# A four-layer graph network on one core: the fourth layer's states in two float32r terms, with edits to the start, the histogram, the reload and the layer ends

## The reference

```
x = layernorm(x + L0)   # mean over incoming edges of (x[src] + rel_emb[type64]) @ W_msg.T + b_msg, plus x @ W_self.T + b_self
x = layernorm(x + L1)   # 4-head attention: exp(att) * weight, summed over dst for each src, then normed per head
x = layernorm(x + L2)   # sum over incoming edges of x[src] @ (W_data or W_control).T, plus self term, relu
x = layernorm(x + L3)   # out[src] += (x[dst] @ W.T + b) / sqrt(deg[src] * deg[dst]), self loops added
```

## Time and profile before

| | us |
|---|---|
| median of 3 runs | 5998.15 (5996.19 to 6017.52) |
| the profiled execution | 5993.14 |
| its span on the core | 5991.4 |
| start, to the first one-hots of the histogram | 73.7 |
| histogram and ranking, with the first projection | 73.7 to 2253.3 |
| reload | 2253.7 to 2273 |
| first layer, shared and own chunks | to 3118 |
| second layer with the softmax step | to 4352 |
| third layer | to 5385 |
| split | to 5401 |
| fourth layer | to 5991 |

### The profile page before, as it was taken

One profiled execution on the slowest core, in us unless ns is written; L12 is line 12 of the kernel. 1 busy time (PEld: TensorE's weight loads), 2 busy tenths in 40 slices (PEclk: granted clock), 3 DMA queues, 4 the chain that ended last, 5 costly groups with the idle time before them and its releaser, 6 DMA issues. The chain is left out here.

```text
span 5991.4 us, 116612 instructions
## 1 busy us (share of the span) xinstructions
PE 5263.6 (88%) x41661; PEld 4183.3 (70%) x41662; DVE 4595.1 (77%) x12723; ACT 1871.7 (31%) x2973; POOL 1532.6 (26%) x1592
## 2 busy tenths in 40 slices
PE   4888888888888876999968999999879999987999
PEld 3666666666666665776748999999856666655666
DVE  7877777777777776878878999999844444447888
ACT  0111111111111113444432333333323333344665
POOL 0577777777777760000000000000000000000000
PEclk9655555555555568999979999999979999998999
DMA  2100000000000002222210000000022222210000
GB/s 81 25 2 2 2 2 2 2 2 2 2 2 2 2 2 99 106 101 101 105 58 3 1 1 1 1 1 1 1 61 82 84 84 82 83 57 5 8 4 10
DMA packets 116663, 190.69 MB, mean 32 GB/s; under 512 B 57855, under 2 KB 60369, under 8 KB 116046
## 3 DMA queue, kind: packets, MB, share of 16 engines
q1 hardware_dynamic: 65070, 179.52, 8.8%
q0 software_dynamic: 50176, 3.31, 0.9%
q10 hardware_dynamic: 1056, 2.86, 0.2%
HBM read 92.34 MB, written 93.22 MB: 31 GB/s over the span
## 5 line engine op out<-in xcount | busy, mean ns | idle before, releaser
L599 POOL DMA_INDIRECT records<-rec,idx x1568 | 1523.5, 972 | 507.6 <-issue 494.3
L1443 ACT ACTIVATE gC<-qC 128x768 bf16<-128x768 f32 (+3 forms) x1176 | 967.7, 823 | 1443.8 <-PE qC L1478 1443.6
L73 DVE TENSOR_TENSOR g<-iota_b,recs 128x768 bf16<-128x768 bf16 (+1 forms) x1970 | 1034.8, 561 | 474.1 <-PE qC L1478 463.7
L1478 PE MATMUL qC<-g 128*128 128x128 f32 (+1 forms) x9628 | 1007.0, 248 | 45.9 <-DVE g L1040 28.3
L1478 PEld LDWEIGHTS qC<-g 128*128 128x128 f32 (+1 forms) x9628 | 904.0, 145 | 156.8 <-DVE g L1040 36.2
L1590 PE MATMUL qO<-X,gC 128*128 128x384 bf16 x4802 | 910.2, 326 | 5.2 <-ACT gC L1443 5.2
L425 DVE SCALAR_TENSOR_TENSOR junk<-pK,key,earlier 128x128 f32<-128x128 f32 (+3 forms) x1568 | 767.1, 544 | 36.4 <-issue 34.5
L511 PE MATMUL pG<-run,hT 49*128 49x98 f32 x3136 | 790.8, 430 | 0.0
L511 PEld LDWEIGHTS pG<-run,hT 49*128 49x128 f32 x3136 | 694.7, 323 | 70.7 <-issue 70.4
L485 PE MATMUL pK<-ident_b,ts_b 128*128 128x128 bf16 x1572 | 379.2, 296 | 326.5 <-DVE junk L425 324.6
L1040 DVE TENSOR_SCALAR g<-iota_f,sl_f,recs 128x128 f32<-128x128 f32 x2413 | 651.4, 340 | 0.0
(11 more groups left out here) (287 smaller groups left out, 5829.0 us busy)
## 6 DMA issues: line engine op xcount, KB each, us to landing
tables<-ring SPq DMA_DIRECT2D x147, 384.0 KB, 2.3
ring<-tables SPq DMA_DIRECT2D x98, 384.0 KB, 3.1
records<-rec,idx POOLq DMA_INDIRECT x1568, 2.1
tables<-ring SPq DMA_DIRECT2D x49, 416.0 KB, 2.4
sl_f<-tables SPq DMA_DIRECT2D x49, 416.0 KB, 3.2
sl_f<-tables SPq DMA_DIRECT2D x49, 384.0 KB, 3.0
records<-null SPq DMA_DIRECT2D x31, 256.0 KB, 9.2
recs<-records SPq DMA_DIRECT2D x1, 4866.0 KB, 14.2
```

Of the source, the lines that this page charges most:

```text
L73: return v.tensor_tensor(o.rearrange("p n (a b) -> p n a b", b=2), iota_b[:, at:at + w].rearrange("p (a b) -> p a b", b=2).unsqueeze(1).br ...
L599: gp.indirect_dma_start(rec_d, bass.IndirectOffsetOnAxis(ap=idx[:, k:k + 1], axis=0), rec[:, k, :], None).then_inc(s_sent[g % 2], 16)
L1443: act.activation(Cs[:, u % 2, 0:n, :], pC[u % 2][:, 0:n, :], ACT.Copy).then_inc(s_cs, 1)
L1478: mm = pe.matmul(pC[u % 2][:, j, :], lhsT, rhs, start=True, stop=True)
```

## The change

It has these parts; line numbers are those of the changed kernel only in the order rows.

1. **Start and histogram.** DVE no longer waits for all five arrays but for src and dst, and makes only what the histogram reads. ACT writes keys and records while the histogram runs; DVE adds types, relations, key and place after its last one-hots.
2. **Reload.** The load of the records and the zeroing of `A` (now on POOL) run beside the first layer's shared chunks. The relation codes are written after those, half on DVE and half on ACT. `X`, `X2` and `rec` share one allocation, `terms`.
3. **First layer.** The relation sum is turned: 64 columns instead of 128, with another operand loaded as weights. The result is transposed by PE and evicted again before the multiplication with the relation table. DVE makes one-hots 3 steps ahead instead of 2.
4. **Layer ends.** No one-hots and no table beyond the last chunk. The recoding takes their place (`recode`), and POOL zeroes the next sums when the last sum is done. The softmax step loses its memset. The shared chunks' records are asked for at once.
5. **Split.** States are cut in two terms of twelve bits (`high_of`, `low_of`): six batches inside the third layer's tail, the last batch after it.
6. **Fourth layer.** Tables are evicted as float32r and multiplied with 256 columns of float32r states (`Xr`); the one-hots and the table product stay bf16.

```diff
+        Xr = nc.alloc_sbuf_tensor_at("Xr", [P, NT, 2, P], F32R, offset=terms_at)
...
-                    v.wait_ge(loads, LOADS)
...
+                    v.wait_ge(ends, 2 * LOAD)
...
+                    place_and_tile(psrc, esrc)
...
                     link(v.tensor_copy(ts_p[:, 0:COLS, :], twice(esrc[:, :], COLS)))
...
+                    place_and_tile(pdst, edst)
...
                     link(v.tensor_copy(td_p[:, 0:COLS, :], twice(edst[:, :], COLS)))
...
+                        v.wait_ge(loads, 3 * LOAD)
+                        v.tensor_scalar(rec_8[:, 0:COLS, B_TYPE], ety2[:, :], 0.0, None, ALU.not_equal)
+                        v.tensor_scalar(rec_8[:, 0:COLS, B_REL], ety64[:, :], 0.0, float(REL - 1), ALU.max, ALU.min)
+                        v.wait_ge(filled, 3)
+                        v.tensor_tensor(key[:, 0:COLS], key[:, 0:COLS], edst[:, :], ALU.add)
+                        v.scalar_tensor_tensor(out=own[:, :], in0=edst[:, :], scalar=float(P), in1=own[:, :], op0=ALU.mult, op1=ALU.add)
...
+                        act.activation(key[:, 0:COLS], esrc[:, :], ACT.Copy, scale=64.0).then_inc(filled, 1)
+                        act.activation(own[:, :], esrc[:, :], ACT.Copy, scale=float(NT * P)).then_inc(filled, 1)
+                        act.activation(ts64_b[:, 0:COLS], esrc[:, :], ACT.Copy, scale=64.0).then_inc(filled, 1)
...
-                    sp.dma_start(recs[:, :, :], records[:, 0:RC, :]).then_inc(s_recs, 16)
-
-                @block.vector
-                def _(v):
-                    v.memset(A[:, :, :], 0.0).then_inc(s_rel, 1)
...
+                            sp.wait_ge(s_block, 16)
+                            sp.dma_start(recs[:, :, :], records[:, 0:RC, :]).then_inc(s_recs, 16)
+
+                        @block.gpsimd
+                        def _(gp):
+                            gp.memset(acc[:, :, :], 0.0).then_inc(s_clear, 1)
...
-                            v.memset(acc[:, :, :], 0.0)
-                            v.scalar_tensor_tensor(out=sl, in0=twice(recs_8[:, :, B_TYPE], RC), scalar=float(P), in1=sl,
-                                                   op0=ALU.mult, op1=ALU.add).then_inc(s_ready, 1)
-                        if mode == "plain":
-                            v.scalar_tensor_tensor(out=sl, in0=twice(recs_8[:, :, B_TYPE], RC), scalar=-float(P), in1=sl,
-                                                   op0=ALU.mult, op1=ALU.add).then_inc(s_ready, 1)
...
+                            v.wait_ge(s_recs, 16)
+                            v.tensor_copy(rel_p[:, 0:MIDDLE, :], twice(recs_8[:, 0:MIDDLE, B_REL], MIDDLE)).then_inc(s_rels, 1)
...
+                        act.dma_start(over[:, :, :], records[:, BUCKETS:BUCKETS + NOB, :]).then_inc(s_block, 16)
...
+                                                for s in range(2):
+                                                    mm = pe.matmul(o_k, Cs[:, par, k, 0:P], Xr[:, bass.ds(As[k], 1), s, :].rearrange("p a w -> p (a w)"),
+                                                                   start=(s == 0), stop=(s == 1))
...
+            parts = 2 if mode == "plain" else 3
...
+            AHEAD = 3 if mode == "relation" else 2
...
+                            gp.wait_ge(s_o, NT * U + PRE)
+                            gp.memset(A1[:, :, 0:XW] if k == 1 else A[:, :, :], 0.0).then_inc(s_wiped, 1)
+                            gp.wait_ge(s_wiped, k)
...
-                            v.memset(h3, 0.0).then_inc(s_blank, 1)
...
+                        def recode():
+
+                            sl = recs_h[:, :, H_SL:H_SL + 2]
+                            v.wait_ge(s_hot, NT * NQ)
+                            if k == 1:
+                                v.tensor_copy(sl_f[:, :], recs_h[:, :, H_SL]).then_inc(s_coded, 1)
+                            if k in (2, 3):
+                                v.scalar_tensor_tensor(out=sl, in0=twice(recs_8[:, :, B_TYPE], RC), scalar=float(P) if k == 2 else -float(P), in1=sl,
+                                                       op0=ALU.mult, op1=ALU.add).then_inc(s_coded, 1)
...
+                        def high_of(b):
+
+                            if b >= RESTS:
+                                v.wait_ge(s_x0, b - RESTS + 1)
+                                v.wait_ge(s_x1, b - RESTS + 1)
+                            v.tensor_scalar(rests[b % RESTS].bitcast(I32), acc[:, b * G7:(b + 1) * G7, 0:P].bitcast(I32), -(1 << 12), None, ALU.bitwise_and).then_inc(s_r, 1)
+
+                        def low_of(b):
+                            v.wait_ge(s_r, b + 1)
+                            v.tensor_tensor(Xr[:, b * G7:(b + 1) * G7, 1, :], acc[:, b * G7:(b + 1) * G7, 0:P], rests[b % RESTS], ALU.subtract).then_inc(s_x1, 1)
...
-                                    make(i, q + 2)
-                                    if q == 0 and i > 0:
+                                    ahead = i * NQ + q + AHEAD
+                                    if ahead < NT * NQ:
+                                        make(i, q + AHEAD)
+                                    if ahead == NT * NQ:
+                                        recode()
...
+                                if k == 3 and (tl, q) in ((2, 5), (2, 6), (2, 7)):
+                                    high_of(q - 5)
+                                if k == 3 and tl >= 3 and (tl - 3) * NQ + q < 2 * (NB - 1) - RESTS:
+                                    u = (tl - 3) * NQ + q
+                                    if u < 2 * (NB - 1 - RESTS):
+                                        low_of(u // 2) if u % 2 == 0 else high_of(u // 2 + RESTS)
+                                    else:
+                                        low_of(u - (NB - 1 - RESTS))
...
-                            act.activation(rel_t[:, :], pR[0:REL, 0:P], ACT.Copy).then_inc(s_rel, 1)
+                            act.activation(rel_t[:, :], pR[:, 0:P // 2], ACT.Copy).then_inc(s_rel, 1)
+
+                        def relations_turned(i):
+                            act.wait_ge(s_relt, i + 1)
+                            act.activation(rel_n[:, :], pE[0:REL, 2 * P:3 * P], ACT.Copy).then_inc(s_reln, 1)
...
+                                for b, when in enumerate(((3, 0), (3, 1), (3, 4), (3, 7), (4, 2), (4, 5))):
+                                    if k == 3 and (tl, q) == when:
+                                        act.wait_ge(s_r, b + 1)
+                                        act.activation(Xr[:, b * G7:(b + 1) * G7, 0, :], rests[b % RESTS], ACT.Copy).then_inc(s_x0, 1)
...
-                                    table(i, u + 1)
+                                    if i * U + u + 1 < NT * U:
+                                        table(i, u + 1)
                                     q = u
+                                    if mode == "relation" and u == 1 and i > 0:
...
-                                            pe.matmul(pR[:, 0:P], h3[:, q % NHB, j, :], h2[:, q % NHB, j, :], start=first, stop=last)
+                                            pe.matmul(pR[:, 0:P // 2], h2[:, q % NHB, j, :], h3[:, q % NHB, j, :], start=first, stop=last)
...
+                        def turn_relations(i):
                             pe.wait_ge(s_rel, i + 1)
                             if i >= 1:
+                                pe.wait_ge(s_reln, i)
+                            pe.transpose(pE[0:REL, 2 * P:3 * P], rel_t[:, 0:REL], ident_f[:, :]).then_inc(s_relt, 1)
...
-                        v.memset(A1[:, :, 0:XW], 0.0)
...
+                        v.tensor_scalar(high[:, :, :].bitcast(I32), A[:, T, 0:P].bitcast(I32), -(1 << 12), None, ALU.bitwise_and).then_inc(s_r, 1)
+                        v.wait_ge(s_r, NB)
+                        v.tensor_tensor(Xr[:, T, 1, :], A[:, T, 0:P], high[:, :, :], ALU.subtract).then_inc(s_x1, 1)
```

191 lines of the change are left out of this document (96 added, 95 removed).

## The result

The changed kernel takes 5870.2 us (median of 4, 5854.9 to 5875.3), the kernel before beside it 6006.2 (median of 4): ratio 0.977, 95% interval 0.974 to 0.980, 2.3% faster. The forecast was 5809 in a range of 5765 to 5875: right in direction, and inside the range by 5 us. The medians fell by 136 us and the profiled span by 138 (5991.4 to 5853.1), where 189 were forecast.

A forecast was written before the change was run, and what follows sets the result against it. PE was taken as late in the fourth and first layers, with DVE next, and other stretches as serial time. The terms summed to -189: 5998 - 189 = 5809 us, range 5765 to 5875.

The forecast's parts named there:

- Fourth layer, -72: Fourth layer's sums: float32r at one column per cycle takes the layer from 535 to 461 us; bounds -85 and -45.
- rival A: Fourth layer: float32r is not one column per cycle; 6016 us at two cycles, 6535 at four; chance 0.08.
- Rival C: Fourth layer: DVE and PE hold each other up, 10 us a tile, -45, total 5836; chance 0.17.
- Rival E: Fourth layer: the clock falls to 1.2 GHz as PE has more gaps, +305, total 6114; chance 0.02.
- First layer, -45: First layer: narrow relation sum and earlier one-hots, less the transpose, save 45 us; bounds -15 and -60.
- three steps ahead removes about 0.4 of the 0.68: First layer, tiles without `node`: one-hots made earlier recover about 0.4 of the 0.68 us PE loses per tile.
- the 0.8 to 1.5 for tiles in which VectorE is late: First layer: tiles in which DVE is late gain from slack only, an estimated 0.8 to 1.5 us each.
- Start, -24: Start and histogram: earlier DVE start and less work before the histogram, more behind it, net -24 us; bounds -20 and -28.
- Reload, -17 and -1.6: Reload: shared chunks' first code comes sooner, -17 us, bounds -12 and -19; the memset before the first one-hots goes, -1.6.
- rival D: Reload and two layer tails: POOL's three memsets block DVE's casts, 14 us in all, total 5823; chance 0.05.
- -10 at the third layer: Start of the third layer: first code at 4355 instead of 4364.97, -10 us.
- Split: Between third and fourth layers: the fourth's first code at 5393.3 instead of 5407.85, -14.6 us; bounds -10 and -17.

The follow-up runs named there:

- the later places: Changed kernel with later node steps in the first and fourth layers, four fourth-layer buffers, wipes on VectorE, empty records beside the histogram: 6562.5 us, ratio 0.970 to the kernel before.

## Why the prediction was right and wrong

- **Fourth layer, -72: right mechanism, a size off: -62.6.** (The forecast's own terms, 535 to 461, give -74, and its bound without bursts -99, not -85.) One cycle per column was nearly so: 0.131 apart for 256 columns, where 0.107 would be the columns alone and rival A began at 0.21. At 0.114 taken, the tile was to be ScalarE's; it is TensorE's, 9.17 for 8.9. The bursts cost 2.95 + 1.52 a batch, 4.5 as against 4.2. Rival C does not hold: quiet tiles are TensorE's, and the mean of the 48 is 9.7, not 10. Rival E, chance 0.02, did not come at 256 columns; with 128 the clock stood at 0.50 all through.
- **First layer, -45: got -18.3. The step that failed** is "three steps ahead removes about 0.4 of the 0.68", with the 0.8 to 1.5 for tiles in which VectorE is late. The 0.68 was read as a wait for one-hots. TensorE's rows of a quiet tile before the change show another cause: six tables and the product with `relw` take 0.94 from the first table to the next relation sum, where six tables alone take 0.35, so 0.59 of the 0.68 stand at the product:

```profile
2369.65 0.51 PE L1478 MATMUL qC<-X,g 128*128 128x128 bf16 x6
2370.18 0.49 PE L1602 MATMUL qE<-relw,rel_t 64*128 64x129 f32 x2
2370.59 0.23 PE L1588 MATMUL qR<-X 128*128 128x128 bf16 x1
...
2371.91 0.51 PE L1478 MATMUL qC<-X,g 128*128 128x128 bf16 x6
2372.26 0.22 PE L1588 MATMUL qR<-X 128*128 128x128 bf16 x1
```
  After the change there are two such places, 0.97 together: the transpose costs 0.38 and not 0.3, and the third step ahead gives 0.05. So a quiet tile fell by 0.88 and not by 1.1. The narrow sum was sized well: 0.192 apart, 0.026 per chunk for 0.021. The other tiles decided: those that VectorE fills gained 0.12 and 0.02, since TensorE's saving is idle time there, and the fifth of a batch lost 0.4 to 1.6 through ScalarE's waits and the clock behind them. In all the third step cost 9.1. Two steps ahead, the change of this layer would have been 755.9 to 727.7, -28; with the later places it is -44. That this is the forecast's number is chance: the forecast did not see that the places matter, and had no term for the clock here.
- **Start, -24: got -21.** The 39 us for the first one-hots missed SyncE's issues, which the prediction had not looked at. The sizes of VectorE's own work held (27.4 and 38.7 for 27 and 38.3).
- **Reload, -17 and -1.6: -18.1**, with 2.1 us of rival D inside it.
- **Layer ends.** -10 at the third layer became -6.2: 2.1 for the blocked scaling, and the code now waits 3.2 for the records where the recoding used to hide that (its first cast came 7.9 sooner, the first halving 6.2; the 1.7 between have no tested cause). The first tail lost 3.8: 0.6 by hops, 3.2 by the memset. Split 13.1 of 14.6 and 2 (the forecast's terms for it add up to 14.3).
- **Why the sum fell at the range's end:** the misses had one sign. Most were work that lost its cover or gained a neighbour (VectorE beside SyncE's issues, scalings beside memsets, evictions behind a wait). The misses add to 50 us; the 2.2 of the ranking among them have no cause that was tested. The wide range, and not the first layer's term, kept the time inside it, by 5 us.

## What to carry to other kernels

When engines run in order and each has its small steps at fixed places in a pipelined loop, a deeper lead on one engine moves its steps later for all others: change the depth and the places together, and read the waits of the engine in between and the granted clock of the stage. When a serial stretch gets shorter, list every queue that ended under it; one of them is next. A narrower operation is not surely cheaper: look at the granted clock before its time is read.
